# Two-layer attention network on one core: the second layer's value projection moves from the first layer's loop into the second's, and the first layer's instruction orders are laid out anew

## The chip, the core and the metric

The kernel runs on one core of a Trainium2 chip. A core has five engines with instruction streams of their own: TensorE (PE, matrix products and transposes into the eight PSUM banks), VectorE (DVE), ScalarE (ACT), GpSimd (POOL) and SyncE (SP, which here only issues DMAs). They run in parallel and meet at semaphores; each engine works through its own list strictly in order, so an instruction that waits holds up all behind it. The metric is the device time of one execution in microseconds, lower is better.

## The reference

32 independent sequences of 128 tokens with 128 features go through two layers. All is fp32.

```python
x = x + xattn0(layernorm(x), ctx)      # 16 heads of 8, key mask, biases
x = x + moe(layernorm(x))              # top-2 of 8 experts, 128 -> 512 -> 128, relu
x = x + xattn1(layernorm(x), ctx)      # 16 heads of 64, query mask:
#   k, v = split(ctx @ Wkv);  q = x @ Wq;  softmax(q k^T / 8 + mask) v @ Wout + bout
x = x + ffn(layernorm(x))              # 128 -> 512 -> 128, relu, biases
```

`v = ctx @ Wkv[:, 1024:]` of the third line is the second layer's value projection: for each sequence a product of the 128x128 context with a 128x1024 matrix. It depends on the context alone, not on `x`, and so can be computed at any time.

## The kernel before

The rows of `x` stay in SBUF for the whole run (`X`, 32 tiles of 128x128). There are three phases.

**Phase 0, the first layer's attention and the router.** Each engine runs `step0(n, p)` from `over_steps`, a software pipeline: at step n, parts of several sequences stand in one list. `p` is the parity of n and picks one of two buffers. The steps in the middle are loops of two steps per iteration, cut into four loops between which `late_loads` issues bulk weight loads on SyncE. For a sequence the chain is: normalise (`norm_*`, GpSimd does the power of -1/2), transpose (`transpose_in`, bank 5, read to `XCT` by `read_xct` on ScalarE), project to keys and queries (`project`, bank 4), split both into a high and a low part (`PARTS`; `kh`, `kl` and `ql` on VectorE, `qh` on ScalarE), write them to DRAM and read them back in a block layout (`KBD`, `QS`; SyncE), four score groups of four heads (`scores`, lines 1042 and 1045, banks 0 and 1 in turn), row maxima (line 748), exponentials with row sums (line 580), transpose of the probabilities (`transpose_unit`, line 1027, banks 2 and 3 in turn, read by `read_PT` on VectorE, line 759, and ScalarE, line 588), 16 value products (`values`, line 1057), scaling by the reciprocal sums (`RB`, `RTS`, `OT0`, line 851), output projection (line 1140), residual sum (line 857). The router then normalises the row alone (`XND`), transposes it, computes expert logits, top-8, index and one-hot (`lgs`, `top8`, `topi`, `tope`, `hot1`, `chosen`), counts places (`place`, `next_row`), and GpSimd scatters the normalised rows (copied to `XK`) to DRAM, line 519.

In the same loop the second layer's value projection is computed: `second_layer_v(f)`, line 1074, two matmuls of 128x512 per sequence into bank 6. ScalarE copies each half to `V_OUT` (`read_v_half`, line 595) and SyncE writes the 512 KB to the DRAM tensor `second_layer_values` (line 410). The two halves stand in TensorE's list behind the second score group and behind the third; both use bank 6, so the second waits for ScalarE's copy of the first.

**Phase 1, the experts**, over the scattered rows. **Phase 2, the second layer**, `step1(n, p)` with the same kind of pipeline: 16 key and query projections (`project_y`, line 1192, banks 4 to 6), scores in two groups (line 1206), row maxima, exponentials, scaling on GpSimd (line 316), transposes, values (line 1225, banks 5 and 6), output projection (line 1275, bank 7), and the feed-forward part (lines 1263 and 1280, both bank 4). SyncE reads the stored values of each sequence back to `V1` (line 454).

The order of instructions on each engine is written out by hand in `step0` and `step1`. The semaphores used below are named after what they count: `a["e"]` exponential groups, `a["pv"]` value groups, `a["qh"]` high parts of queries, and so on.

Of the kernel before, what the change touches and what calls it, by code (L numbers as in the profile page):

```python
# [20 lines left out]
FP32 = mybir.dt.float32  # L21
# [69 lines left out]

def is_first(n):
    return isinstance(n, int) and n == -1
# [9 lines left out]
def build(nc, x, ctx_in, mask_keys, mask_queries, wq0, bq0, wk0, bk0, wv0, bv0, wo0, bo0,  # L103
          gate_w, moe_w1, moe_w2, wq1, wkv1, wout1, bout1, ffn_w1, ffn_b1, ffn_w2, ffn_b2, out, c_dram, xs, ys):
    ctx = ExitStack()
    with ctx:  # L106
# [6 lines left out]
        v_dram = nc.dram_tensor("second_layer_values", (NB, P, INNER), FP32, kind="Internal").ap()  # L113
# [68 lines left out]
        V_OUT = wide[:, PAIRS:2 * PAIRS, :].rearrange("p k s -> p (k s)")  # L182
# [52 lines left out]
        wq_scaled, ld_kv = sem("wq_scaled"), sem("ld_kv")  # L235
# [14 lines left out]
        a = names("a", common + "kq v0 qc qh ql kc kh kl kw qw vc qs bd s mx e rd rb t pt0 pt1 pv rt rts oN o x pj pjv vst")  # L250
        c = names("c", common + "mask0 mask1 v0 v1 y yc s mx e rd nm t pt0 pt1 pv oT o x")
# [78 lines left out]
        def _(sp):  # L330
# [4 lines left out]
            def early_loads(n):  # L335

                if n == -3:
# [6 lines left out]
                    sp.dma_start(wv1[:], wkv1[:, INNER:]).then_inc(ld_kv, 16)  # L344
# [13 lines left out]
            def late_loads(k):  # L358
# [20 lines left out]
                if k == 4:  # L379
                    sp.dma_start(wout[:], wout1.rearrange("(c p) d -> p c d", p=P)).then_inc(ld_w1, 16)  # L380

            def step0(n, p):

                if exists(n + 1):
                    m = n + 1
                    if isinstance(n, int) and m < 2:
                        sp.wait_ge(bd_zeroed, m + 1)
                    wait_apart(sp, (a["kw"], 16 * (m + 1)), (a["s"], NU * (m - 1)))
                    for j in range(G):
                        rows = spread(1 - p, 1).rearrange("(g j x) s -> j x g s", g=NU, j=G)[j]  # L390
                        sp.dma_start(KBD[32 * j:32 * j + 32, 1 - p, :, j, :].bitcast(FP32), rows).then_inc(a["bd"], 16)
                    wait_apart(sp, (a["qw"], 32 * (m + 1)))
                    sp.dma_start(QS[:, 1 - p, :, :].bitcast(FP32),
                                 spread(1 - p, 0).rearrange("(g x) s -> x g s", g=NU)).then_inc(a["qs"], 16)
                if exists(n + 3):
                    load_ctx(sp, a, n + 3, 1 - p)
                if isinstance(n, int):
                    early_loads(n)
                if exists(n + 2):
                    m = n + 2  # L400
                    wait_apart(sp, (a["kl"], m + 1), (a["bd"], 16 * G * (m - 1)))
                    sp.dma_start(spread(p, 1).rearrange("(c o i) s -> c o i s", o=2, i=2),
                                 PARTS[:, 0:2, :].unsqueeze(1).broadcast_to([P, 2, 2, P])).then_inc(a["kw"], 16)
                    wait_apart(sp, (a["ql"], m + 1), (a["qs"], 16 * (m - 1)))
                    for o in range(2):
# [903 lines left out]
```

## Time and profile before

| | us |
|---|---|
| three runs, median (lowest, highest) | 1075.23 (1074.84, 1075.88) |
| the profiled execution, its own time | 1078.77 |
| its span, first to last instruction | 1076.9 |

| engine | busy us | share of the span |
|---|---|---|
| PE (matmul) | 942.5 | 88% |
| PEld (weight load, beside PE) | 805.1 | 75% |
| DVE | 671.6 | 62% |
| ACT | 596.2 | 55% |
| POOL | 416.6 | 39% |

A line of a timeline shows the start in us, the length in us, the engine, the line of the kernel, the operation, what is written and read, how many instructions were merged, and in brackets the idle time before it and what ended it. Records overlap, as an engine starts an instruction before the last one has left its pipeline; what an instruction costs its engine is therefore the distance between starts. An fp32 matmul has two records. "<-issue" stands for time in which the profile shows no releaser.

### The profile page before, as it was taken

The numbers are of one execution on the slowest core, as the hardware profiler recorded it, in microseconds if no ns is written. First come the engines' busy times: TensorE is split into PE (matmuls) and PEld (weight loads), VectorE is DVE, ScalarE is ACT, GpSimd is POOL, SyncE is SP. The second block draws the span as 40 slices with busy tenths as digits, with TensorE's granted clock in tenths as the row PEclk, the third lists the DMA queues.
The fourth block names the chain that finished last, engine by engine and source line by source line (L and its number), as shares of the span: only waits on it lengthen the run. The fifth ranks groups of instructions, "written<-read, shape, count | busy, mean of one in ns | idle before, by whom it ended". The sixth has DMA issues, their size and how long they took to land. (4 is left out here: it accounts for less than half of the span.)

```text
span 1076.9 us, 30219 instructions
## 1 busy us (share of the span) xinstructions
PE 942.5 (88%) x8590; PEld 805.1 (75%) x8590; DVE 671.6 (62%) x2173; ACT 596.2 (55%) x2537; POOL 416.6 (39%) x670
## 2 busy tenths in 40 slices
PE   5888788888888873799995799999999999999987
PEld 3556566555665652799995688999999999999986
DVE  5667767767777666122222667777777777777763
ACT  2867777767777670133331455556555655555552
POOL 4123333333333333011113455555555555555531
PEclk9989999989999895799997899999999999999998
DMA  5764475554754522122222011111111111111110
GB/s 152 223 196 148 132 234 163 181 151 132 232 167 139 149 93 62 44 69 68 69 68 71 30 56 51 45 56 59 59 56 56 59 41 52 59 59 59 56 45 9
DMA packets 110658, 103.56 MB, mean 96 GB/s; under 512 B 11759, under 2 KB 96563, under 8 KB 110614
## 3 DMA queue, kind: packets, MB, share of 16 engines
q1 hardware_dynamic: 102958, 89.14, 26.9%
q0 software_dynamic: 5776, 12.99, 3.8%
q10 hardware_dynamic: 1880, 0.92, 0.3%
q8 instruction: 19, 0.31, 0.1%
q14 instruction: 25, 0.20, 0.1%
HBM read 56.45 MB, written 46.56 MB: 96 GB/s over the span
## 5 line engine op out<-in xcount | busy, mean ns | idle before, releaser
L580 ACT ACTIVATE PR<-bank,nmx 128x128 f32<-128x128 f32 x1024 | 362.4, 375 | 130.3 <-issue 114.5
L580 ACT ACTIVATION_READ_ACCUMULATOR PR<-bank,nmx 128x1 f32 x1024 | 218.4, 213 | 0.0
L748 DVE TENSOR_REDUCE nmx<-bank 128x4 f32<-128x512 f32 x256 | 170.0, 685 | 69.8 <-PE bank L1045 60.4
L316 POOL TENSOR_TENSOR PR<-PR,rden 128x512 f32<-128x512 f32 x128 | 134.0, 1047 | 92.5 <-DVE rden L753 91.5
L1027 PE MATMUL bank<-ident,PR 128*128 128x128 f32 x1024 | 152.5, 277 | 0.3 <-DVE YT L759 0.3
L1027 PEld LDWEIGHTS bank<-ident,PR 128*128 128x128 f32 x1024 | 121.0, 143 | 29.9 <-issue 25.9
L1192 PE MATMUL bank<-XCT,wqk 128*128 128x128 f32 x1024 | 123.8, 281 | 0.9 <-ACT XCT L572 0.9
L1192 PEld LDWEIGHTS bank<-XCT,wqk 128*128 128x128 f32 x1024 | 120.6, 197 | 1.6 <-ACT XCT L572 1.6
L572 ACT ACTIVATE XCT<-bank 128x256 f32<-128x256 f32 x64 | 24.7, 385 | 160.9 <-PE bank L1019 160.9
L1074 PE MATMUL bank<-wv,XCT 128*128 128x512 f32 x128 | 74.2, 663 | 37.9 <-ACT wide L595 37.9
L649 ACT ACTIVATE H<-bank 128x512 f32<-128x512 f32 x70 | 41.9, 598 | 107.5 <-PE bank L1162 107.5
L519 POOL DMA_INDIRECT expert_inputs<-wide,scat_idx x64 | 66.0, 1032 | 79.2 <-DVE scat_idx L824 69.1
L917 DVE COPY YT<-bank 128x512 f32<-128x512 f32 x128 | 85.6, 687 | 10.5 <-PE bank L1192 7.8
L276 POOL TENSOR_SCALAR veps<-mv 128x1 f32<-128x1 f32 x128 | 29.0, 226 | 160.0 <-DVE mv L292 100.6
L1206 PE MATMUL bank<-YT 64*128 64x128 f32 x1024 | 74.8, 286 | 6.5 <-ACT PR L580 2.8
L550 POOL DMA_INDIRECT QF<-expert_outputs,gidx x64 | 65.5, 1024 | 36.5 <-POOL gidx L547 24.4
L279 POOL TENSOR_TENSOR rstd<-veps,expo 128x1 f32<-128x1 f32 x128 | 73.3, 572 | 15.7 <-POOL veps L276 10.2
L1045 PE MATMUL bank<-KBD,QS 128*128 128x512 f32 x128 | 76.6, 599 | 0.0
L1206 PEld LDWEIGHTS bank<-YT 64*128 64x128 f32 x1024 | 62.5, 188 | 15.6 <-issue 10.9
L1162 PE MATMUL bank<-PR,w 128*128 128x128 f32 x560 | 70.1, 279 | 0.5 <-DVE PR L900 0.5
L1169 PE MATMUL bank<-w,H 128*128 128x128 f32 x560 | 69.3, 278 | 0.0
L533 POOL DMA_DIRECT2D expert_outputs<-PR x35 | 19.1, 545 | 128.7 <-DVE PR L908 128.7
(178 smaller groups left out, 1810.2 us busy)
## 6 DMA issues: line engine op xcount, KB each, us to landing
second_layer_values<-wide SPq DMA_DIRECT2D x32, 512.0 KB, 2.8
wide<-second_layer_values SPq DMA_DIRECT2D x32, 512.0 KB, 3.3
expert_outputs<-HF SPq DMA_DIRECT2D x32, 256.0 KB
expert_outputs<-HF SPq DMA_DIRECT2D x64, 128.0 KB
KBD<-expert_outputs SPq DMA_DIRECT2D x128, 64.0 KB
QS<-expert_outputs SPq DMA_DIRECT2D x32, 256.0 KB
PR<-expert_inputs SPq DMA_DIRECT2D x36, 128.0 KB, 2.1
expert_outputs<-PR POOLq DMA_DIRECT2D x35, 128.0 KB, 2.0
```

What stands on the lines that cost most here:

```text
L279: nc.gpsimd.tensor_tensor(rstd[:, p, :], veps[:, p, :], expo[:], ALU.pow).then_inc(s["rstd"], 1)
L316: nc.gpsimd.tensor_tensor(unit, unit, rden[:, p, G * g:G * g + G].unsqueeze(2).broadcast_to([P, G, P]), ALU.mult).then_inc(s["nm"], 1)
L580: last = nc.scalar.activation(PR[:, g, j * P:(j + 1) * P], S_BANK[g % 2][:, j * P:(j + 1) * P], ACT.Exp, bias=nmx[:, p, h:h + 1], accum_ou ...
L748: nc.vector.tensor_reduce(nmx[:, p, G * g:G * g + G], S_BANK[g % 2][:].rearrange("p (j k) -> p j k", j=G), AXX, ALU.max, negate=True).then ...
L917: nc.vector.tensor_copy(YT[:, q, G * g:G * g + G, :].rearrange("p h s -> p (h s)"), Y_BANK[g][:]).then_inc(c["yc"], 1)
L1027: last = nc.tensor.transpose(T_BANK[g % 2][:, j * P:(j + 1) * P], PR[:, g, j * P:(j + 1) * P], ident[:])
L1045: mm(S_BANK[g % 2][:], QS[:, p, g, :], KBD[:, p, g, :, :].rearrange("p j s -> p (j s)"), start=False, stop=True, skip_group_check=True).th ...
L1074: mm(bank[6][:], XCT[:, q, 1, :], wv1[:, 512 * f:512 * f + 512], start=True, stop=True).then_inc(a["pj"], 1)
L1162: last = mm(bank[k][:, i * P:(i + 1) * P], w1[:, e, i * P:(i + 1) * P], XT[:, k, :], start=True, stop=True)
L1169: last = mm(bank[4 + k][:, 0:P], H[:, k, i, :], w2[:, e, i, :], start=(i == 0), stop=(i == HC - 1))
L1192: last = mm(Y_BANK[g][:, j * P:(j + 1) * P], wqk1[:, 1 - g // 2, chunk * P:(chunk + 1) * P], XCT[:, q, 1 - g // 2, :], start=True, stop=True)
L1206: mm(S_BANK[r][:, j * P:(j + 1) * P], QT1[half, p, chunk, :], KT1[half, p, chunk, :], start=(j == 0), stop=False, skip_group_check=True)
```

## The change

- The second layer's value projection leaves phase 0 with its two matmuls, two ScalarE copies, the DRAM tensor, its write and its semaphores. Phase 2 gets it: `project_v(half)` writes bank 5 and bank 6, and ScalarE's `read_v(half)` copies them to `V1`. The read from DRAM goes. The weights `wv1` are loaded after the last cut of phase 0.
- In phase 2 the feed-forward's second product moves from bank 4 to bank 7, ahead of the output projection, which then waits for `d["x"]`; the second score group stands behind the transposes of the first unit.
- Phase 0 gets new orders on all five engines. For sequence n the output projection, the residual sum and the router's transpose go to a later step; ScalarE's step begins with the query part, `RTS`, the third and fourth exponentials and a transposed unit of the sequence before; ScalarE and SyncE run three steps longer.

The diff, cut to its core (TensorE's, ScalarE's and SyncE's loop bodies and phase 2):

```diff
@@ SyncE, step0
+                    wait_apart(sp, (a["ql"], n + 2), (a["qs"], 16 * (n)))
+                    for o in range(2):
+                        sp.dma_start(spread(q, 0).rearrange("(c o i) s -> o c i s", o=2, i=2)[o],
+                                     PARTS[:, 2 + o, :].unsqueeze(1).broadcast_to([P, 2, P])).then_inc(a["qw"], 16)
...
-                if exists(n + 1):
-                    wait_apart(sp, (a["pjv"], 2 * n + 4))
-                    sp.dma_start(v_dram[n + 1], V_OUT).then_inc(a["vst"], 16)
@@ ScalarE, step0 after the change
+                if exists(n + 1):
+                    act.wait_ge(a["qc"], n + 2)
+                    wait(act, a["qw"], 32 * (n + 1))
+                    nc.scalar.activation(PARTS[:, 2, :].bitcast(FP32R), QC, ACT.Copy).then_inc(a["qh"], 1)
+                if exists(n - 2):
+                    act.wait_ge(a["rt"], n - 1)
...
+                if exists(n - 1):
+                    exponentials(a, n - 1, q, 2)
+                    exponentials(a, n - 1, q, 3)
+                    read_PT(a, n - 1, 1)
...
+                if exists(n + 2):
+                    read_xct(a, n + 2, p, True, a["v0"], n + 1)
                 if exists(n):
                     exponentials(a, n, p, 0)
                     exponentials(a, n, p, 1)
...
-                if exists(m):
-                    read_v_half(m, 0)
                 if exists(n - 1):
                     read_PT(a, n - 1, 3)
@@ ScalarE, step1
                 if exists(n):
                     exponentials(c, n, p, 3)
+                if exists(m):
+                    read_v(0)
+                if exists(n):
                     read_PT(c, n, 1)
+                if exists(m):
+                    read_v(1)
@@ TensorE, step0: the new order, waits left out
+                    nc.tensor.transpose(M_BANK[:, 0:P], XND[:], ident[:]).then_inc(rt["tr"], 1)
...
+                    mm(M2_BANK[:, 0:P], OT0[:, p, :], wo0T[:], start=True, stop=False)
...
+                    scores(n, p, 0)
...
+                    mm(bank[4][:, 2 * P:3 * P], XCT[:, p, 1, :], wv0T[:], start=True, stop=False)
...
+                    transpose_in(a, n + 2, p, True)
+                if exists(n):
+                    scores(n, p, 1)
+                if exists(n - 1):
+                    transpose_unit(a, n - 1, 2)
...
-                if exists(m):
-                    second_layer_v(0)
@@ TensorE, step1
+                def project_v(half):
+
+                    if exists(n - 1):
+                        wait(pe, c["oT"], 2 * (n - 1) + half + 1)
+                    else:
+                        pe.wait_ge(c["yc"], NU * m + half + 2)
+                    mm(bank[5 + half][:], XCT[:, q, 1, :], wv1[:, 512 * half:512 * half + 512], start=True, stop=True).then_inc(c["v"], 1)
...
+                if exists(m):
+                    project_v(0)
                 if exists(n):
                     transpose_unit(c, n, 1)
-                if exists(n - 1):
+                if exists(n - 2):
+                    wait(pe, d["hr"], n - 1)
+                    wait(pe, d["xct"], n - 1)
+                    for kk in range(HC):
+                        mm(bank[7][:, 0:P], H[:, 0, kk, :], f2[:, kk, :], start=(kk == 0), stop=False)
...
+                if exists(m):
+                    project_v(1)
+                if exists(n - 1):
+                    wait(pe, c["oT"], 2 * n)
                     if exists(n - 2):
-                        wait(pe, d["xct"], n - 1)
+                        wait(pe, d["x"], n - 1)
```

VectorE's new order in phase 0, in words: router transpose copy (`XDT`), residual sum, input statistics, row maxima 0, reciprocal of the sums, statistics of the residual, row maxima 1, `place` and `next_row`, transposed unit 2, `KC`, `picked`, high and low part of the keys, `lgs`, `QC`, top-8, `XND`, index search, row maxima 2, low part of the queries, `slot_f`, `XN`, `tope` and `hot1`, row maxima 3, `scat_idx`, `OT0`, transposed unit 0, `chosen`. GpSimd's: `RB`, router normalisation, copy to `XK`, input normalisation, two scatters.

## Rows read from the trace of the kernel before

**Rows 1.** Windows (stretch, length, busy PE PEld DVE ACT POOL, clock, DMA share, GB/s): both layers.

```profile
21.30:394.40 373.10, 308.68 (x2353) 222.84 (x2354) 259.37 (x993) 280.36 (x1236) 119.67 (x230) 0.97 0.57 172
...
584.00:1076.90 492.90, 471.98 (x4896) 428.20 (x4896) 341.01 (x926) 260.50 (x1184) 248.94 (x347) 0.97 0.16 51
```

**Rows 2.** Windows of 25 sequences each: PE, PEld, DVE, ACT, POOL, clock, DMA.

```profile
101.00:401.00 300.00, 247.45 (x1932) 179.36 (x1928) 210.40 (x833) 225.42 (x992) 102.51 (x195) 0.98 0.54 163
640.00:1000.00 360.00, 359.19 (x3813) 327.55 (x3813) 264.71 (x722) 203.11 (x925) 197.29 (x275) 1.00 0.17 55
```

**Rows 3.** Timeline of PE in the second layer: the first score group of two steps.

```profile
797.97 1.16 PE L1206 MATMUL bank<-YT 64*128 64x128 f32 x16
...
812.38 1.16 PE L1206 MATMUL bank<-YT 64*128 64x128 f32 x16
```

**Rows 4.** Timeline of DVE in one step of the first layer: its waits.

```profile
310.53 0.69 DVE L748 TENSOR_REDUCE nmx<-bank 128x4 f32<-128x512 f32 x1 [0.30 <-PE bank L1045]
...
318.04 0.69 DVE L748 TENSOR_REDUCE nmx<-bank 128x4 f32<-128x512 f32 x1 [1.42 <-PE bank L1045]
...
320.51 0.29 DVE L851 TENSOR_TENSOR OT<-bank,RTS 128x128 f32<-128x128 f32 x1 [0.29 <-PE bank L1057]
...
321.95 0.29 DVE L857 TENSOR_TENSOR X<-bank,X 128x128 f32 x1 [0.89 <-PE bank L1141]
322.28 0.69 DVE L748 TENSOR_REDUCE nmx<-bank 128x4 f32<-128x512 f32 x1
```

**Rows 5.** Timeline of PE around that step of the first layer.

```profile
311.52 1.02 PE L1074 MATMUL bank<-wv,XCT 128*128 128x512 f32 x2
312.38 0.38 PE L1066 MATMUL bank<-XCT,wqkT 128*128 128x128 f32 x2
...
315.77 1.13 PE L1074 MATMUL bank<-wv,XCT 128*128 128x512 f32 x2 [1.14 <-ACT wide L595]
316.73 0.60 PE L1027 MATMUL bank<-ident,PR 128*128 128x128 f32 x4
...
317.93 1.97 PE L1057 MATMUL bank<-YT 128*64 128x128 f32 x32
319.83 0.66 PE L1027 MATMUL bank<-ident,PR 128*128 128x128 f32 x4
...
321.30 0.44 PE L1140 MATMUL bank<-wo0T,OT 128*128 128x128 f32 x2
```

**Rows 6.** Timeline of ACT in that step.

```profile
315.12 0.60 ACT L595 ACTIVATE wide<-bank 128x512 f32<-128x512 f32 x1
...
316.09 0.37 ACT L580 ACTIVATE PR<-bank,nmx 128x128 f32<-128x128 f32 x1
...
317.37 0.23 ACT L580 ACTIVATION_READ_ACCUMULATOR PR<-bank,nmx 128x1 f32 x1
```

**Rows 7.** Timeline of SyncE: the reads of the block layout.

```profile
319.43 1.86 SPq L391 DMA_DIRECT2D KBD<-expert_outputs  x4
321.46 0.39 SPq L393 DMA_DIRECT2D QS<-expert_outputs  x1
```

**Rows 8.** Timeline of POOL: second scatter of a step, and the copy behind it.

```profile
318.81 0.96 POOL L519 DMA_INDIRECT expert_inputs<-wide,scat_idx  x1 [0.30 <-issue]
322.06 0.29 POOL L524 COPY wide<-XND 128x128 f32<-128x128 f32 x1 [2.29 <-DMA expert_inputs<-wide,scat_idx]
```

**Rows 9.** Waits from 101 to 401 us: total, times, longest.

```profile
POOL wide L524 <- DMA expert_inputs<-wide,scat_idx: 65.3, 25, 6.3
```

**Rows 10.** Timeline of ACT: one instruction per step, around the longest step.

```profile
203.88 0.31 ACT L608 ACTIVATE HF<-QF 128x128 fp32r<-128x128 f32 x1 [0.16 <-DVE QF L797]
...
218.79 0.31 ACT L608 ACTIVATE HF<-QF 128x128 fp32r<-128x128 f32 x1 [3.17 <-DVE QF L797]
```

**Rows 11.** Windows around a fall of the granted clock, columns as above.

```profile
215.00:218.00 3.00, 0.63 (x4) 0.66 (x4) 1.02 (x6) 0.62 (x4) 1.27 (x4) 0.72 1.20 183
218.00:221.00 3.00, 2.13 (x4) 0.80 (x4) 2.49 (x11) 2.21 (x9) 0.79 (x2) 0.50 0.16 36
```

More of the change, by code:

```diff
@@ L89, in loads, with is_sequence, upto @@
     return 8 * (m - p) + 16
+def is_sequence(k, m):
+    return isinstance(m, int) and m == k
+def upto(m, each=1, item=0):
+    count = each * m + item + 1
+    return min(count, each * NB) if isinstance(m, int) else count
 def is_first(n):
@@ L652, in step1, with read_v @@
                 q, m = 1 - p, n + 1
+                def read_v(half):
+                    act.wait_ge(c["v"], 2 * m + half + 1)
+                    wait(act, c["pv"], NU * (m - 1))
+                    nc.scalar.activation(V1[:, q, 8 * half:8 * half + 8, :], bank[5 + half][:].rearrange("p (h d) -> p h d", h=8),
+                                         ACT.Copy).then_inc(c["vc"], 1)
                 def read_heads(half):
@@ L762, in step0 @@
             def step0(n, p):
-                q, l = 1 - p, n + 2
+                q = 1 - p
                 if isinstance(n, int):
                     weights_and_masks(n)
+                if exists(n - 3):
+                    dve.wait_ge(rt["tr"], n - 2)
+                    wait(dve, rt["lg"], n - 3)
+                    nc.vector.tensor_copy(XDT[:], M_BANK[:, 0:P]).then_inc(rt["xct"], 1)
+                if exists(n - 2):
+                    dve.wait_ge(a["o"], n - 1)
+                    xrow = X[:, bass.ds(n - 2, 1), :].rearrange("p o d -> p (o d)")
+                    nc.vector.tensor_tensor(xrow, M2_BANK[:, 0:P], xrow, ALU.add).then_inc(a["x"], 1)
+                if exists(n + 3):
+                    norm_dve_stats(dve, a, None, n + 3, q)
+                if isinstance(n, int) and n == -2:
+                    bias_rows()
                 if exists(n):
@@ L970, in step1 @@
                     norm_dve_stats(dve, c, None, n + 2, p)
+                if exists(n - 2):
+                    dve.wait_ge(d["y"], n - 1)
+                    wait(dve, out_stored[p], loads(n - 4, p))
+                    nc.vector.tensor_tensor(acc[:, p, :], bank[7][:, 0:P],
+                                            X[:, bass.ds(n - 2, 1), :].rearrange("p o d -> p (o d)"),
+                                            ALU.add).then_inc(d["x"], 1)
                 if exists(n + 2):
@@ L1015, in transpose_in @@
                     pe.wait_ge(s[f"ctx{p}"], loads(m, p))
[L1016 removed]
+                if m_free is not None:
+                    wait(pe, m_free, m_count)
                 last = nc.tensor.transpose(M_BANK[:, 0:P], XN[:, p, :], ident[:])
@@ L1078, in step0 @@
+                    mm(bank[4][:, 2 * P:3 * P], ones3[:], brow[:, 0, :], start=False, stop=True).then_inc(a["v0"], 1)
+                if exists(n + 2):
+                    wait(pe, a["x"], upto(n - 2))
+                    if isinstance(n, int):
+                        wait(pe, a["rts"], upto(n - 2))
+                        wait(pe, a["xct"], upto(n + 1))
+                    transpose_in(a, n + 2, p, True)
+                if exists(n):
+                    scores(n, p, 1)
                 if exists(n - 1):
@@ L1102, in step0 @@
+                    nc.tensor.transpose(M2_BANK[:, 2 * P:3 * P], RB[:], ident[:]).then_inc(a["rt"], 1)
+                if exists(n - 3):
+                    pe.wait_ge(rt["xct"], n - 2)
+                    wait(pe, rt["next"], upto(n - 4))
+                    if isinstance(n, int):
+                        wait(pe, rt["xct"], upto(n - 3))
+                        wait(pe, rt["lgc"], upto(n - 4))
                     mm(M_BANK[:, 0:NE], XDT[:], gw[:], start=True, stop=True).then_inc(rt["lg"], 1)
```

332 lines of the change are left out of this document (137 added, 195 removed).

## The prediction

> **What bounds the kernel now.** I read the stages first, because one average over the span would mix them. Cut at the first and last sequence's first score group and at the start of the second layer, the table of stretches gives 373.1 us for 31 sequences of the first layer (12.04 us each) and 492.9 us for the second layer, ends included [rows 1]. The steady part of each is in [rows 2]: 25 sequences lie in each of its stretches.
>
> The second layer is bound by TensorE: 359.19 of 360 us busy, at full clock [rows 2]. Busy time of matmuls is modelled, so I checked it by starts: the same matmul group starts at 797.97 and 812.38, a step of 14.41 us [rows 3], and the steps between differ by a few hundredths. The other engines are busy 264.71/25 = 10.6 us (VectorE), 8.1 (ScalarE) and 7.9 (GpSimd) per sequence [rows 2].
>
> The first layer is bound by no engine alone. Per sequence TensorE is busy 247.45/25 = 9.9 us, ScalarE 9.0, VectorE 8.4, GpSimd 4.1 [rows 2]. So I read the timelines of one step for what each engine waits on. VectorE's step from 310.53 to 322.28 is 11.75 us, and three waits on TensorE stand in it: 1.42, 0.29 and 0.89 us, 2.60 in all [rows 4]. That leaves 9.15 us of work and short waits on VectorE's own results. The step before it reads the same way: 12.25 us with five waits of 3.40 us in all, so 8.85. The mean is 9.0. The largest wait (row maxima of the fourth score group) has its cause in TensorE's timeline: the second half of the second layer's value projection waits 1.14 us for ScalarE to copy the first half out of its only bank [rows 5], and that copy stands behind the copy of the query part in ScalarE's order. The fourth scores are queued behind that matmul.
>
> **The change part by part.**
>
> *Second layer, added work.* Each sequence gains two matmuls of 128x512 in fp32. In the trace the pair of records of one half takes 0.86 us from start to next start (311.52 to 312.38), 0.96 where it follows an idle engine (315.77 to 316.73) [rows 5]. So 2 x 0.86 = 1.72 us per sequence. They land on the engine that has no hole: 14.41 becomes 16.13. The first projection stands in the prologue (about +1.5 us, as the first scores are behind it) and the second in a hole while the first sequence's exponentials end; I count 30 x 1.72 + 1.5 = 53.1. The two copies added to ScalarE (0.49 us each: such a copy and a second one of its size take 315.12 to 316.09 from start to next start [rows 6]) make it 8.1 + 1.2 = 9.3 us busy in 16.1 (0.60 us of record each): covered, if each is done when its bank is wanted. The first half's bank (bank 5) still holds the attention output of the previous sequence; its copy follows the third group of exponentials, and I work it out to end within 0.1 us of when TensorE comes to it. The feed-forward output now goes to bank 7 ahead of the output projection; its hidden activations are ready about when TensorE arrives, since the added half-projection and one transpose unit stand between. I take 0 to 0.1 us a step for both, 2 us in all. At the end of the layer the last output projection now waits for the one-but-last feed-forward sum: +1 us. Sum for the second layer: +53 + 2 + 1 = **+56 us**, bounds +52 (nothing but the matmuls of 30 steps) and +63 (0.3 us of wait in each step).
>
> *Second layer, removed.* The read of 512 KB per sequence from DRAM, with its issue on SyncE, is gone. No engine waits for it in the steady part: **0**. DMA is busy a share of 0.17 there [rows 2].
>
> *First layer, removed work.* Per sequence 1.72 us of TensorE, two copies of ScalarE (1.0 us of issue), one DMA of 512 KB. TensorE has at most 9.9 - 1.7 = 8.2 us left, ScalarE 8.0. The 1.42 us wait of VectorE on the fourth scores has no cause any more. If that were all, the step would be 12.0 - 1.5 = 10.5 us.
>
> *First layer, new orders.* They take the projection of the output, the residual sum and the router's transpose one step later, and put the third and fourth exponentials of a sequence at the head of ScalarE's next step. What this does to VectorE's other waits (0.29 for the head outputs, 0.89 for the residual [rows 4]) I worked out by walking one step of the new orders over all engines with the old durations. Start at the second group of exponentials of sequence n, time 0. It is read out at 1.5 (316.09 to the end at 317.60 [rows 6]); ScalarE copies the transposed unit 3 of n-1 until 2.0; the 16 value matmuls run 1.90 us (317.93 to 319.83 [rows 5]) to 3.9; VectorE can scale the head outputs at 4.2 (0.29 us), and it comes to that instruction at about 4.5, so it does not wait. The output projection gives the residual at 0.65 us from its start (321.30 to 321.95 [rows 4, 5]), at about 5.5; VectorE is busy until then with the copy of transposed unit 0, `chosen` and `XDT`. Input statistics (0.5) and the row maxima of n+1 (0.69 each) follow. Through TensorE and ScalarE alone this ring closes in 8.1 us. VectorE's own list is longer: the 9.0 us found above, minus about 0.2 us of waits on its own results, which are now filled by other instructions (top-8 and index search), is 8.8. So VectorE is the next bound. I add 0.2 for waits that the walk can't see (the rings of 8.1 and 8.8 are close). Step: **9.0 us**, bounds 8.6 (work without self-waits, 8.4, and 0.2) and 10.5 (only the value wait is gone).
>
> Queues that instructions are moved past. SyncE: the query part's write now stands ahead of the reads of the K layout in the next step, and waits for VectorE's last part. The reads are issued from 319.43 to 321.29 and the read of Q at 321.46 [rows 7]; with an estimate of 2.3 to 4 us for each landing, the lower end from the scatter's [rows 8], I find Q in place some 2 to 3 us before the scores want it. GpSimd: the copy of the normalised rows waits until the scatter before has landed, 2.3 us after its issue ends (318.81 + 0.96 to 322.06 [rows 8]). VectorE's next normalisation waits for that copy. This ring is 2.4 us of scatter issue, 0.3 of copy, 2.9 of VectorE's list from `XND` to `scat_idx` and the landing: 7.9 us, under 9.0. But the longest such wait was 6.3 us [rows 9], which makes the ring 11.9 us; it comes where bulk weights are loaded. I therefore keep the lengthened steps of before as they are: five steps of 12.8 to 14.9 us exceed 11.85 us by 9.6 us in all; the longest is 203.88 to 218.79 [rows 10]. About 4 us more are VectorE's own set-up steps (mask rows, zeroing), which were partly hidden and are not when it is the bound.
>
> Sum of the first layer: 31 x 9.0 + 9.6 + 4 = 292.6 against 373.1: **-80 us** (rounded). The start (query write behind the row moves, +0.5) and the drain (same chain of router steps) I take as 0 within 2 us.
>
> *Total:* -80 + 56 = -24. The profiled run took 1078.8 us and the median is 1075.2, 0.3% less; the difference is carried to the median: 1075.2 - 24 = **1051 us**.
>
> *A rule weighed.* TensorE stands still for 1.14 us in a step and the clock stays up: 0.97 of full speed over the first layer [rows 1]. It fell to 0.72 and 0.50 only in 215 to 221 us, after a stretch in which TensorE was busy 0.63 of 3 us [rows 11]. The Trainium skill, "TensorE: Matmul & The Clock Gate", section "Why this matters for your kernels", warns against idle gaps between bursts of matmuls, as the array falls back to half clock. That speaks against taking work from a layer with idle TensorE. It is a rival below; the sum goes by the row, since the new step is shorter and TensorE's share of it is not lower: by distances of starts it is occupied 8.8 of 12 us, and 7.1 of 9 without the projection.
>
> **The rivals.**
>
> A. *The new orders gain only the value wait.* Another wait replaces the two others: scatter ring, K/Q round trip, or register arithmetic ahead of waits. Step 10.5 us: 31 x 10.5 + 13.6 = 339, -34 us; total +22: **1097 us**. It decides from a step of 9.79 us on, where 31 x 9.79 + 13.6 = 317 gives back all 56 us. For it: the rings of 7.9, 8.1 and 8.8 us lie close, and a landing of 4 us makes the scatter ring 9.6. Against it: typical landings were 2.3 us with more DMA traffic than will be left. Steps of 9.8 and more: 0.19.
>
> B. *Step shorter than 8.7*, VectorE without self-waits and fewer lengthened steps: 31 x 8.5 + 10 = 273.5, -100; total -44: **1031 us**. 0.06.
>
> C. *The projection is cheap in the second layer.* Weight loads keep their unit busy 327.55 of 360 us [rows 2], 1.30 us free per step. If that were the room, 1.72 us would cost 0.42, or 13 us in all: 1075.2 - 80 + 13 + 3 = **1011 us**. Against it: matmuls start back to back. 0.02. The rule behind it is in the Trainium skill, "Perfetto Trace Analysis", section "Identifying the Most-Contended Engine": headroom of TensorE is judged by the load of weights, not by matmul busy time.
>
> D. *Half clock in the first layer.* TensorE's 7.1 us become 14.2, a step of about 14.5: 31 x 14.5 + 13.6 = 463, +90; total +146: **1221 us**. By the gate's rule above; the trace shows such drops only after long stops. 0.02 (inside the slower cases).
>
> **How the numbers follow.** Forecast, step 8.7 to 9.4: 1042 to 1064, chance 0.58. Step 9.4 to 9.75: 1064 to 1075, 0.13, of which 0.04 is within 0.2% (2 us), about what a measurement of this kernel can tell from no change. A with D: 0.21 slower. B and C: 0.08. Faster 0.58 + 0.09 + 0.08 = 0.75, same 0.04, slower 0.21. The range leaves out B's lower half and C below (0.05), and the upper half of A with D above (0.13): **1032 to 1088**.
>
> **What would show it.** The second layer's step 16.1 to 16.3 us with TensorE busy throughout; a hole at the half-projections means the banks came late. The first layer's step 9.0 us with VectorE idle under 0.5 us of it. VectorE waiting at the normalisation for GpSimd means the scatter ring, at row maxima 0 and 2 for scores means the exponentials or the K/Q round trip; TensorE's granted clock under 0.9 in the first layer means D. The prediction is wrong if two of VectorE's waits stay, or if the walk missed a wait on the same engine pair in the other direction.

## The result, and the profile after

The change makes the kernel faster: 1036.69 us (median of 4 runs, 1036.06 to 1037.69) against 1075.46 (4 runs, 1074.84 to 1075.88), a ratio of 0.9641, 95% interval 0.9624 to 0.9658. The forecast was 1051 us, 14 us too high, within its range of 1032 to 1088. The profiled execution took 1036.79 us with a span of 1035.2.

Where the 41.7 us of span between the two profiled executions went, cut at VectorE's first and last scaling of head outputs (`OT0`) and at the second layer's first `XCT` copy:

| stretch | before | after | difference |
|---|---|---|---|
| start to first `OT0` | 41.25 | 37.69 | -3.6 |
| first to last `OT0`, 31 steps of the first layer | 371.7 | 279.4 | -92.3 |
| last `OT0` to second layer (router's end, experts) | 173.7 | 173.1 | -0.7 |
| second layer to the end | 490.2 | 545.1 | +54.9 |

The page of the changed kernel gives, engine by engine, busy us, share of the span and number of instructions:

```profile
PE 936.0 (90%) x8590; PEld 800.7 (77%) x8590; DVE 661.9 (64%) x2173; ACT 586.9 (57%) x2537; POOL 415.6 (40%) x670
```

The second layer is still bound by TensorE. Windows of the changed kernel (columns as in [rows 1]); the first is 200 us of the first layer, the second has the stretch of [rows 2]:

```profile
101.00:301.00 200.00, 182.24 (x1602) 143.19 (x1602) 175.42 (x734) 168.33 (x828) 91.07 (x172) 0.97 0.57 169
640.00:1000.00 360.00, 357.04 (x3472) 307.28 (x3468) 237.18 (x641) 205.61 (x875) 170.31 (x237) 1.00 0.05 15
```

The timeline of PE shows both half-projections (L1182) in their places with no wait in the whole step; it is 784.60 - 768.45 = 16.15 us long, against 14.41 in [rows 3]:

```profile
762.18 1.16 PE L1268 MATMUL bank<-XDT,f 128*128 128x128 f32 x8
763.20 1.12 PE L1182 MATMUL bank<-wv,XCT 128*128 128x512 f32 x2
764.16 0.60 PE L1024 MATMUL bank<-ident,PR 128*128 128x128 f32 x4
764.60 1.11 PE L1278 MATMUL bank<-f,H 128*128 128x128 f32 x8
765.55 0.22 PE L1279 MATMUL bank<-brow,ones 128*128 128x128 bf16 x1
765.60 1.08 PE L1182 MATMUL bank<-wv,XCT 128*128 128x512 f32 x2
766.52 1.95 PE L1289 MATMUL bank<-wout,wide 128*128 128x128 f32 x16
...
768.45 1.16 PE L1210 MATMUL bank<-YT 64*128 64x128 f32 x16
...
784.60 1.16 PE L1210 MATMUL bank<-YT 64*128 64x128 f32 x16
```

In the first layer the waits of [rows 4] are gone from the usual step. The same stretch of VectorE's list, from the scaled heads (L846) over the residual (L768) to the row maxima, two steps' maxima 8.34 us apart (the next pair is 8.52 apart, 8.43 on average), has no bracket. From 101 to 301 us VectorE waits 2.8 us for scores, in six pieces, and 13.0 us for GpSimd's copy of the normalised rows, also in six:

```profile
248.64 0.28 DVE L846 TENSOR_TENSOR OT<-bank,RTS 128x128 f32<-128x128 f32 x1
248.84 0.68 DVE L754 COPY YT<-bank 128x512 f32<-128x512 f32 x1
249.43 0.16 DVE L851 TENSOR_TENSOR chosen<-hot 128x8 bf16<-128x8 f32 x1
249.51 0.29 DVE L764 COPY XDT<-bank 128x128 f32<-128x128 f32 x1
249.71 0.28 DVE L768 TENSOR_TENSOR X<-bank,X 128x128 f32 x1
249.91 0.28 DVE L277 BATCH_NORM_STATS2 stats<-X 128x6 f32 x1
250.28 0.18 DVE L279 BATCH_NORM_AGGREGATE mv<-stats 128x2 f32<-128x6 f32 x1
250.41 0.69 DVE L743 TENSOR_REDUCE nmx<-bank 128x4 f32<-128x512 f32 x1
...
258.75 0.69 DVE L743 TENSOR_REDUCE nmx<-bank 128x4 f32<-128x512 f32 x1
```

Four steps between 100 and 300 us are long: 11.1, 11.2, 12.0 and 11.4 us. POOL's timeline shows why in the longest. The copy of the normalised rows (L513) waits 4.56 us for the scatter to land, and VectorE's next `XND` waits for that copy; the window says what else was moving, 301 GB/s with the DMA engines 0.94 busy, just behind a block of weight loads. The write of the keys' and queries' parts is late by the same block (ScalarE's copy of the query part waits 2.63 us for it), but that wait ends at 227.50 us, before the scatter's:

```profile
221.22 0.96 POOL L521 DMA_INDIRECT expert_inputs<-wide,scat_idx  x1 [0.30 <-issue]
...
227.97 0.29 POOL L513 COPY wide<-XND 128x128 f32<-128x128 f32 x1 [4.56 <-DMA expert_inputs<-wide,scat_idx]
```

```profile
219.00:228.00 9.00, 8.26 (x75) 6.22 (x73) 5.60 (x23) 6.34 (x32) 3.17 (x6) 1.00 0.94 301
```

Behind this stop the granted clock falls. TensorE is busy 0.33 us of the three from 228 to 231 us, and then runs at half clock:

```profile
231.20:234.20 3.00, 2.90 (x12) 2.47 (x12) 2.59 (x11) 2.28 (x11) 2.07 (x2) 0.50 0.54 156
```

The same is read behind the other three long steps (0.50 at 122, 177 and 286 us), and the step behind each takes 9.0 to 9.7 us in place of 8.59.

### The profile page after: what moved, and what is told of

It reads as the page before. It is cut to its first block and busy times, and to the rows that moved or that the text cites. A ratio compares the mean times of both kernels' runs of the same rounds, so it can differ in the third digit from the quotient of the medians.

```text
span 1035.2 us, 29985 instructions
## 1 busy us (share of the span) xinstructions
PE 936.0 (90%) x8590; PEld 800.7 (77%) x8590; DVE 661.9 (64%) x2173; ACT 586.9 (57%) x2537; POOL 415.6 (40%) x670
## 5 line engine op out<-in xcount | busy, mean ns | idle before, releaser
L578 ACT ACTIVATION_READ_ACCUMULATOR PR<-bank,nmx 128x1 f32 x1024 | 223.4, 218 | 0.0
L1196 PE MATMUL bank<-XCT,wqk 128*128 128x128 f32 x1024 | 121.6, 278 | 0.9 <-ACT XCT L570 0.9
L1196 PEld LDWEIGHTS bank<-XCT,wqk 128*128 128x128 f32 x1024 | 118.4, 194 | 1.6 <-ACT XCT L570 1.6
L521 POOL DMA_INDIRECT expert_inputs<-wide,scat_idx x64 | 66.0, 1032 | 97.7 <-DVE scat_idx L841 86.8
L285 POOL TENSOR_SCALAR veps<-mv 128x1 f32<-128x1 f32 x128 | 29.2, 228 | 165.5 <-DVE mv L301 150.6
L1042 PE MATMUL bank<-KBD,QS 128*128 128x512 f32 x128 | 78.7, 615 | 0.0
L1289 PEld LDWEIGHTS bank<-wout,wide 128*128 128x128 f32 x512 | 61.9, 192 | 15.8 <-issue 13.7
L1182 PE MATMUL bank<-wv,XCT 128*128 128x512 f32 x128 | 70.0, 630 | 1.0 <-ACT wide L648 1.0
```

Source lines behind the costliest of these rows:

```text
L521: nc.gpsimd.indirect_dma_start(xs, bass.IndirectOffsetOnAxis(scat_idx[:, p, k:k + 1], 0), XK[:, p, :], None).then_inc(rt[f"sc{p}"], 16)
L578: last = nc.scalar.activation(PR[:, g, j * P:(j + 1) * P], S_BANK[g % 2][:, j * P:(j + 1) * P], ACT.Exp, bias=nmx[:, p, h:h + 1], accum_ou ...
L1042: mm(S_BANK[g % 2][:], QS[:, p, g, :], KBD[:, p, g, :, :].rearrange("p j s -> p (j s)"), start=False, stop=True, skip_group_check=True).th ...
L1182: mm(bank[5 + half][:], XCT[:, q, 1, :], wv1[:, 512 * half:512 * half + 512], start=True, stop=True).then_inc(c["v"], 1)
L1196: last = mm(Y_BANK[g][:, j * P:(j + 1) * P], wqk1[:, 1 - g // 2, chunk * P:(chunk + 1) * P], XCT[:, q, 1 - g // 2, :], start=True, stop=True)
```

## The experiments

Three groups of four runs; each group ran on one chip beside the kernel before. "Steps" is first to last `OT0`, 31 steps; "usual" their median; "long" is the excess over the median of the steps more than 0.5 us above it; "2nd" the mean step of the second layer's steady part. Of the changed kernel one execution lies outside the groups, and one is in group 3; groups 1 and 2 have none beside them, so their comparisons with it cross groups.

| run | group | time us | ratio to before (95%) | steps | usual | long | 2nd |
|---|---|---|---|---|---|---|---|
| before | | 1075.46 | | 371.7 | 11.70 | 12.7 | 14.41 |
| changed | | 1036.69 | 0.9641 (0.9624, 0.9658) | 279.4 | 8.59 | 16.8 | 16.15 |
| value_only | 1 | 1110.71 | 1.036 (1.0298, 1.0422) | 354.3 | 10.72 | 29.2 | 16.15 |
| orders_only | 1 | 1009.05 | 0.9408 (0.9354, 0.9461) | 304.7 | 9.24 | 21.9 | 14.40 |
| v_half | 1 | 1053.41 | 0.981 (0.9749, 0.9872) | 293.0 | 8.71 | 26.6 | 16.15 |
| late_loads | 1 | 1035.88 | 0.9659 (0.9604, 0.9714) | 277.3 | 8.71 | 9.0 | 16.15 |
| dve_extra | 2 | 1054.02 | 0.9796 (0.9748, 0.9844) | 285.3 | 8.84 | 15.4 | 16.5 |
| act_extra | 2 | 1052.90 | 0.9786 (0.9745, 0.9826) | 283.4 | 8.83 | 14.4 | 16.5 |
| half_projection | 2 | 1052.20 | 0.9787 (0.9738, 0.9836) | 282.6 | 8.81 | 14.7 | 16.3 |
| orders_fine | 2 | 1005.33 | 0.933 (0.93, 0.9359) | 296.8 | 9.75 | 1.7 | 14.40 |
| changed again | 3 | 1040.06 | 0.9697 (0.9674, 0.9721) | 281.9 | 8.80 | 15.2 | 16.15 |
| dve_two | 3 | 1047.82 | 0.9778 (0.9738, 0.9817) | 291.3 | 9.15 | 13.8 | 16.15 |
| orders_again | 3 | 1006.01 | 0.9385 (0.9362, 0.9409) | 301.2 | 9.23 | 19.4 | 14.40 |
| orders_fine_again | 3 | 992.83 | 0.9253 (0.9223, 0.9283) | 286.3 | 9.23 | 3.7 | 14.40 |

### The two parts apart: value_only and orders_only

`value_only` takes `second_layer_v`, `read_v_half` and the DRAM write out of the old `step0` and gives it the changed `step1`. `orders_only` is the changed `step0` with the two matmuls, two ScalarE copies and a write per step, and the old `step1`:

```diff
@@ value_only, TensorE's old step0 (ScalarE and SyncE likewise)
-                if exists(m):
-                    second_layer_v(0)
...
-                if exists(m):
-                    second_layer_v(1)
@@ orders_only, TensorE's new step0
+                    pe.wait_ge(a["pjv"], 2 * n + 1)
+                    mm(bank[6][:], XCT[:, p, 1, :], wv1[:, 512:1024], start=True, stop=True).then_inc(a["pj"], 1)
                     scores(n, p, 0)
...
+                    wait(pe, a["pjv"], 2 * (n + 1))
+                    mm(bank[6][:], XCT[:, q, 1, :], wv1[:, 0:512], start=True, stop=True).then_inc(a["pj"], 1)
                 if exists(n):
                     scores(n, p, 2)
```

> The value projection alone is moved to the second layer as in the changed kernel; the first layer keeps the orders of the kernel before, with the projection, its copies and its write taken out. Theory (each engine's order sets the step): TensorE still waits for ScalarE's value copy and VectorE's list still has its gaps, so the first layer's step is about 10.5 us against 12.04 before and 8.43 in the changed kernel (mean without lengthened steps), the second layer's step 16.15; total about 1097 us. Rival (the orders are worth nothing, the removed work did it all): step about 8.5, total about 1037 us, the same as the changed kernel.

> The changed kernel's first-layer orders, but both halves of the second layer's value projection stay in the first layer (through a bank of their own, copied by ScalarE, written to DRAM), and the second layer is that of the kernel before. Theory (lists): TensorE gets 2 x 0.86 us and ScalarE 2 x about 0.6 us per step on top of a step of 8.43, in which each had 0.5 to 1.3 us to spare, so the step goes to 9.0 to 9.3 us; the second layer's step is again 14.41; total 1036.7 - 55 + 31 x 0.7 = about 1003 us, 33 us below the changed kernel. Rival (the orders only work once the projection is out): the step stays above 10.5 us, total about 1046 us, above the changed kernel.

With the old orders the usual step falls only to 10.72 us, 16.5 us more than before is lost in long steps, and the projection's 55 us in the second layer are not earned back: 1110.71 us, slower than before by 3.6%. That is rival A's condition (orders that gain nothing else), and 14 us beyond its price; the waits are others than the three it names. TensorE waits for VectorE at the router's bank, and VectorE for TensorE at the scores and the residual (101 to 380 us; engine, line, waited for, total, times, longest), and the granted clock from 101 to 301 us is 0.92:

```profile
PE bank L1083 <- DVE next_row L774: 34.7, 24, 5.1
PE bank L1093 <- DVE lgs L803: 24.9, 23, 1.3
```

```profile
DVE nmx L738 <- PE bank L1035: 28.3, 44, 1.4
DVE X L847 <- PE bank L1120: 22.0, 24, 1.3
```

```profile
101.00:301.00 200.00, 156.24 (x1294) 119.87 (x1290) 147.52 (x589) 136.81 (x654) 73.33 (x138) 0.92 0.47 137
```

The new orders alone give 1009.05 us, better than the whole change. In the third group the same kernel takes 1006.01 us against 1040.06 for the changed kernel beside it: moving the projection costs 34 us on top of the new orders, 19.4 us gained in the 31 steps and 4.0 ahead of them, 57.6 lost in the second layer. TensorE has no gap in a usual step of it (14 us of the first layer):

```profile
217.00:231.00 14.00, 14.00 (x126) 10.75 (x125) 12.70 (x55) 13.27 (x65) 5.33 (x12) 1.00 0.59 198
```

### What a half-projection costs in the second layer: v_half and half_projection

`v_half` computes, stores and reads back heads 0 to 7 in the first layer's way, and drops `project_v(0)`. `half_projection` drops `project_v(1)` and copies half 0 twice; the values of heads 8 to 15 are not computed.

```diff
@@ TensorE, step1: v_half drops the first, half_projection the second
-                if exists(m):
-                    project_v(0)
...
-                if exists(m):
-                    project_v(1)
```

> The changed kernel, with half 0 of the value projection in the first layer (one 128x512 matmul, one ScalarE copy, one DRAM write per step; read back in the second layer) and half 1 in the second. Theory (VectorE's list bounds the first layer's step, with 0.62 us of ScalarE and over 0.86 us of TensorE to spare): first layer's step 8.43 to 8.6 us, so +0 to +5 us there; second layer's step 15.3 (16.15 - 0.86), -27 us there; total 1010 to 1015 us. Rival (TensorE or ScalarE bounds the first layer's step as closely as VectorE does): step 9.0 or more, total 1027 us or more.

> The changed kernel, but the second layer projects only half 0 of the values and copies it twice, so that heads 8 to 15 get the wrong values: the second 128x512 matmul of each step is left out, the copies stay. It is the mirror of the run that kept half 1 and left half 0 out, whose step stayed at 16.15 us because TensorE then waited 0.78 us for VectorE's relu where half 0 had stood. Theory (half 0 covers that wait, half 1 covers nothing): the second layer's step falls by the whole 0.86 us to 15.3, total about 1037 - 27 = 1010 us. Rival (something else holds the second layer's step at 16.15, and no matmul less helps): total about 1037 us.

Both theories on the second layer fell. Without half 0 its step stays at 16.15 us: TensorE reaches the feed-forward's second product (here L1300) 0.86 us earlier and waits 0.78 us there for VectorE's relu:

```profile
763.35 1.16 PE L1292 MATMUL bank<-XDT,f 128*128 128x128 f32 x8
764.34 0.60 PE L1041 MATMUL bank<-ident,PR 128*128 128x128 f32 x4
765.73 1.16 PE L1300 MATMUL bank<-f,H 128*128 128x128 f32 x8 [0.78 <-DVE H L974]
```

Without half 1 it is 15.95 us in its undisturbed steps: the output projection comes early to bank 7, which VectorE's feed-forward sum (L968) has not read yet:

```profile
723.92 1.12 PE L1278 MATMUL bank<-f,H 128*128 128x128 f32 x8
724.87 0.22 PE L1279 MATMUL bank<-brow,ones 128*128 128x128 bf16 x1
725.57 0.68 PE L1287 MATMUL bank<-wout,wide 128*128 128x128 f32 x4 [0.48 <-DVE QF L968]
```

So each half-projection covers a wait that shows in the changed `step1` when it is taken out: the two together cost 1.74 us a step against the old order, and either one beside the other 0.00 or 0.20 us. No run has the changed `step1` with neither half, or the old one with one half; by TensorE's work the latter would take 14.41 + 0.86 = 15.3 us (an estimate), so what `v_half` could have gained with another `step1` stays open.

In the first layer `v_half`'s usual step of 8.71 us, between the 8.59 and 8.80 of the changed kernel, shows that TensorE and ScalarE had room for one half. Its long steps cost 10 us more, and their waits are of another kind: ScalarE cannot overwrite `V_OUT` before the values' write to DRAM has landed (12.0 us from 101 to 301 us).

```profile
ACT wide L603 <- DMA second_layer_values<-wide: 12.0, 5, 3.3
```

### What bounds the first layer's step: dve_extra, act_extra, dve_two and a control

```diff
                     row_max(a, n, p, 1)
+                    nc.vector.tensor_copy(wide[:, 16:20, :], ident[:].unsqueeze(1).broadcast_to([P, 4, P]))   # dve_two: twice
```
```diff
+                    nc.scalar.activation(wide[:, 20:24, :], ident[:].unsqueeze(1).broadcast_to([P, 4, P]), ACT.Copy)
                     exponentials(a, n - 1, q, 2)
```

> The changed kernel with one more VectorE instruction in each first-layer step: a 128x512 copy from SBUF to an unused SBUF buffer, after the maximum of group 1, that nobody waits for. Theory (VectorE's list sets the first layer's step, since it shows no idle time there): every step grows by what the copy takes, about 0.6 us as the 128x512 copies of the trace, so 32 x 0.6 = +19 us; total about 1056 us. Rival (TensorE and VectorE are both near the bound and some waiting is hidden in VectorE's packed records): growth well under half, total below 1046 us.

> The changed kernel with one more ScalarE instruction in each first-layer step: a 128x512 copy from SBUF to an unused SBUF buffer, ahead of the exponentials of group 2, where ScalarE waits 0.62 us in every step. Theory (VectorE bounds, ScalarE has that gap): the copy takes about 0.5 us and fills the gap, total 1037 to 1040 us. Rival (ScalarE's exponentials lie on the ring that sets the step): +0.5 us in each step, +16 us, total about 1053 us.

> The changed kernel unaltered, on the chip of the three runs below, as their control: the runs with one extra instruction, and with half a projection, all showed every second step of the second layer at 16.9 us where the changed kernel's first profile has 16.28, and a first-layer step of about 8.8 us against 8.59, whatever had been edited. If that belongs to the execution and not to the edits, this run can show it too (1045 to 1050 us); if it belongs to the edits, this run is at 1037 us again, with 16.28 and 8.59.

> As the run with one extra VectorE copy per first-layer step (0.33 us of VectorE's time), but with two such copies, 0.66 us. Theory (VectorE's list of 8.4 to 8.5 us bounds the step, with at most 0.25 us of waiting in it): the step is 9.05 to 9.2 us, 0.45 to 0.6 above the control of this call, the first layer 14 to 19 us longer. Rival (the step is set by a ring through TensorE and VectorE, which has room for what is put beside it): step under 0.3 us above the control, first layer under 9 us longer.

The totals of group 2 are misleading: in all three kernels derived from the changed one every second step of the second layer was longer (in `act_extra` 16.81 us in place of 16.15 between starts of TensorE's first score group). `dve_extra` and `act_extra` do not touch that code, and their second layers take 553.5 and 555.2 us to the end, against 545.2 in the control of group 3. The last section says what the traces of group 2 have in common. The first layers of the group can be compared with each other. Against `half_projection`, whose first layer is the changed kernel's, the ScalarE copy added 0.8 us to 31 steps: it has room, as the theory said, though the total of 1052.90 us reads like the rival's. One VectorE copy (0.33 us from start to start, not the 0.6 I expected of it) added 2.8 us. That neither theory foresaw, and the waits of `half_projection` say why: VectorE waited there for TensorE's counts, 0.23 us at a time, at just the place of the copy (120 to 300 us). These counts (L1098) came 0.9 us after their matmul's record had ended; in the control of group 3 they came 0.03 us after it, and VectorE waits there twice, 0.4 us in all. So the room that the copy found belongs to group 2.

```profile
DVE place L784 <- PE bank L1098: 4.2, 18, 0.6
```

Two copies against the control: usual step 9.15 against 8.80, so 0.35 us for 0.67 of copies, and the 31 steps +9.5 us, just above the rival's 9 and short of the theory's 14 to 19. VectorE is then full:

```profile
249.80 0.69 DVE L743 TENSOR_REDUCE nmx<-bank 128x4 f32<-128x512 f32 x1
...
254.04 0.42 DVE L782 COPY wide<-ident 128x512 f32<-128x512 f32 x1
254.38 0.41 DVE L783 COPY wide<-ident 128x512 f32<-128x512 f32 x1
254.71 0.15 DVE L786 TENSOR_TENSOR place<-bank,next_row 128x8 f32<-128x8 f32 x1
...
258.94 0.69 DVE L743 TENSOR_REDUCE nmx<-bank 128x4 f32<-128x512 f32 x1
```

9.14 us less the two copies (254.04 to 254.71, 0.67) is a list of 8.47 us. The changed kernel's usual step lies 0.1 to 0.3 us above it; in the control these are waits of `XND` for GpSimd's copy, 14 in the 200 us against 4 with the two copies, ten of the 14 being of 0.2 to 0.5 us (control first, then dve_two; total, times, longest):

```profile
DVE XND L308 <- POOL wide L513: 13.6, 14, 3.5
```

```profile
DVE XND L308 <- POOL wide L513: 8.1, 4, 2.5
```

So VectorE's list is the floor, as forecast, and the ring through the scatter lies 0.1 to 0.3 us above it.

### The long steps: late_loads, orders_fine and its repeat

`late_loads` moves the calls of `late_loads(k)`, all but the load of `X`, behind SyncE's last step, with the loop cut as before. `orders_fine` is `orders_only` with a cut at every iteration and a piece of the loads at each:

```diff
@@ late_loads
-            over_steps(sp, step0, -3, NB + 3, 3, 4, late_loads)
+            over_steps(sp, step0, -3, NB + 3, 3, 4, first_loads)
+            for k in range(5):
+                late_loads(k)
@@ orders_fine
-    cuts = list(range(loop_start, loop_end, 3)) + [loop_end] if between else [loop_start, loop_end]
+    cuts = list(range(loop_start, loop_end, every)) + [loop_end] if between else [loop_start, loop_end]   # SyncE: every=1
+                if 1 <= k <= 8:
+                    sp.dma_start(w1[:, k - 1, :], moe_w1[k - 1]).then_inc(ld_ffn, 16)
+                    sp.dma_start(w2[:, k - 1, :, :], moe_w2[k - 1].rearrange("(c p) d -> p c d", p=P)).then_inc(ld_ffn, 16)
```

> The changed kernel, but the bulk loads of the expert, feed-forward and second-layer weights, which SyncE issues between its stretches of the first layer's loop, are all issued after the last first-layer step; the cuts of the loop stay. Theory (the lengthened steps come from the loads, which slow the scatter and the spreads): the steps of 9.2 to 12.4 us fall to 8.4 to 8.6, first layer 281.6 to about 266 us; the expert stage may start up to 15 us later, since its weights come late. Rival (the cut of the loop itself costs the time): the lengthened steps stay where they are and the first layer keeps 281 us.

> The kernel with the changed first-layer orders and the value projection in the first layer (1009.05 us), and SyncE's bulk loads cut into eleven pieces of about 0.5 MB, issued every two steps, in place of four blocks of 1 to 2 MB every six. Theory (a block of loads delays the landing of the scatter, and only a delay of several us outlasts the slack of the row buffer): the lengthened steps of 10.5 to 15.2 us, 21.9 us above the usual 9.24 in all, lose over half of that: first layer about 12 us shorter, total 995 to 999 us. Rival (the same bytes cost the same time wherever they are put): total about 1009 us.

> The kernel with the changed first-layer orders and the value projection in the first layer once more, beside the control. If the chip of this call gives the same step as before (9.24, TensorE without a gap), total 1007 to 1010 us, 28 us or more below the control. If its step goes to 9.5 to 9.8 us, the 9.75 us of the run with finely cut loads belongs to the chip and not to the loads.

> The same with the bulk loads cut into eleven pieces, on the same chip as the run before it. Theory (fine loads take away the lengthened steps and cost nothing else): 12 us or more below the run with the loads in four blocks. Rival (the bytes cost the same spread or in a block, since the run of the other call had no lengthened step but 9.75 us in every step): within 4 us of it.

`late_loads`: the four long steps between 100 and 300 us fall to 8.2 to 9.0 us, so the loads made them and not the cuts, and the granted clock there is 1.00 in place of 0.97. But the total is unchanged, and the 31 steps take 277.3 us against 279.4, where the theory had 15 us less: the usual step is 8.71, the long step near the start stays (13.1), the block now meets the last two scatters, whose steps take 11.4 and 10.7 us, and the second layer starts 3 us later after the last heads:

```profile
301.59 0.29 POOL L518 COPY wide<-XND 128x128 f32<-128x128 f32 x1 [4.48 <-DMA expert_inputs<-wide,scat_idx]
...
313.32 0.29 POOL L518 COPY wide<-XND 128x128 f32<-128x128 f32 x1 [4.82 <-DMA expert_inputs<-wide,scat_idx]
```

With the projection in the first layer the long steps have a second cause beside the scatter. In `orders_again` ScalarE waits for the values' write behind a block, 4.17 us at most, and TensorE and VectorE wait behind it:

```profile
ACT wide L603 <- DMA second_layer_values<-wide: 12.0, 3, 4.2
```

Cut finely, the loads cost almost nothing. In group 3, side by side, the usual step is 9.23 us with either layout, that wait is 5.7 us in all, the long steps shrink from 19.4 to 3.7 us, and the time from 1006.01 to **992.83 us**, 7.5% below the kernel before and 4.5% below the changed one in that group. TensorE is busy 197.98 of 200 us of the first layer at full clock:

```profile
101.00:301.00 200.00, 197.98 (x1663) 153.35 (x1663) 176.06 (x724) 182.07 (x852) 91.36 (x172) 1.00 0.70 222
```

In group 2 the same kernel had 9.75 us in every step and 1005.33 us. Group 3's chip was the same one. What differed in the traces is TensorE's counts (last section): in group 2 the count of the context's transpose (L1022) came 0.6 us after the matmul's record ended, in group 3 0.01 us after it, and only in group 2 did ScalarE wait for it (9.2 us from 101 to 301 us, 18 times). Why the counts were late is open.

## Why the prediction was right, point by point

- **Second layer, +56.** Measured +54.9; step 16.15 us for 16.1 to 16.3. The mechanism held: the work landed on an engine without a gap. The closeness of the sum is partly luck. From first to last first score group the 31 steps grew by 48.2 us (448.8 to 497.0) and the start by 0.2, for the 53.1 of the sum; the banks were in time in every step, so the 2 us of waits did not come; and the end grew by 6.4 us (34.1 to 40.5), for 1. In the last steps, where no projection is left, TensorE waits 0.78 us for VectorE's relu and 0.47 for its feed-forward sum, the same waits that the half-projections cover elsewhere (v_half, half_projection). I had not seen them. The profiled execution of before was itself 2.6 us longer in this stretch than `orders_again`, which runs the same second layer (490.2 against 487.6 us); against that the addition is 57.5 us.
- **First layer's step, 9.0.** Measured 8.43 us where VectorE is packed, 8.59 as the median. The mechanism held (VectorE's list bounds; the waits of [rows 4] go), and the term was mis-sized. I took 9.0 us of list and short waits, subtracted 0.2 for the short waits and added 0.2 for unseen ones; the list itself measures 8.47 (dve_two), so the short waits were worth 0.5, and what lies above the list is 0.12. 31 x 0.41 = 13 us, about the size of the error of the total, though other errors below cancel beside it.
- **Lengthened steps, 9.6 us as before.** They cost 16.8. Four of them come from the scatter behind a block of loads; with a shorter step the same delay sticks out further. That took back 7 us. Behind each of the four the clock was at 0.50 for a stretch, and the next step was 0.4 to 1.1 us longer; the sum has no term for that.
- **Set-up steps +4, start +0.5, drain 0.** The start came 3.6 us earlier and the drain 0.7; no 4 us of set-up show, and the steps under the median give another 3.7. With these the 31 steps come out at 292.6 - 12.7 + 7.2 - 4 - 3.7 = 279.4 us. The medians differ by 38.8 us and not by 41.7, mostly because the profiled execution of before was 3.3 us slower than its median.
- **"If only the removed work counted, 10.5 us."** value_only: 10.72, and 29 us of long steps. The step was right within 0.2 us, but not the reason given for it: waits of VectorE for the scores remain (28.3 us from 101 to 380 us). Rival A's condition, orders that bring nothing else, is just that kernel, and it is slower than before. The new orders were worth 67 us in group 3 (before to orders_again), the removal 19 us.
- **Rival C** fell: the unit that loads weights was busy 307.28 of 360 us and free 2.4 us a step, while TensorE had no gap. The Trainium skill names that unit's busy share as one of two measures of TensorE's headroom ("Perfetto Trace Analysis", section "Identifying the Most-Contended Engine"). Judged by it the added work would have cost the 0.42 us a step of rival C; it cost 1.74, so the runs do not agree.
- **Rival D** did not come as priced: the clock is 0.97 over the first layer, as before. It came in part, behind the long steps. The reading that it was built on was too narrow: in the kernel before the clock was at 0.50 not only around 217 to 223 us but also from 59.5 to 66 and from 363.5 to 369.5 us. In the changed kernel it is at 0.50 behind each of the four long steps, in `late_loads`, without them, 1.00 from 101 to 301 us, and in value_only 0.92, with TensorE busy 156 of 200 us. The Trainium skill warns of idle gaps between bursts ("TensorE: Matmul & The Clock Gate", section "Why this matters for your kernels"); these runs agree in direction.

## What to carry to other kernels

Before moving work off an engine that waits, lay out the orders so that the waits go, and only then ask what the work costs where it stands: here the first was worth 67 us, and the move that came with it lost 34 of them. A matmul that covers a wait is free to keep and worth nothing to remove; read what stands behind it in the same list. Spread bulk loads in pieces over a loop that has a short DMA round trip in its ring; here a block was paid in the ring at both places where it was put. Compare kernels only within a group that has its own control: in one group of this case a disturbance of the executions was as large as the effects under test.

## What was not expected of the hardware

- Behind a block of loads of 2 MB the scatter's second DMA landed 5.8 us after its issue ended, against 2.3 us one step before, at 301 GB/s.
- In group 2 VectorE's copy of the transposed unit 0 waited 0.85 us for TensorE in every second step of the second layer, where the changed kernel's did not wait, with TensorE's instructions before it at the same times. First act_extra, then the changed kernel:

```profile
806.96 0.69 DVE L755 COPY w<-bank 128x512 f32<-128x512 f32 x1 [0.85 <-PE bank L1231]
```

```profile
793.90 0.68 DVE L754 COPY w<-bank 128x512 f32<-128x512 f32 x1
```

It is not the chip (the control of group 3 ran on the same one without it) and not an extra VectorE instruction (dve_two has none of it). The semaphore events of the traces say more. VectorE's copy waits for the first count of the value products (L1231 in act_extra). In act_extra that count came at 806.94, 2.22 us after the first of these matmuls started; in the changed kernel it came 1.10 us after. From 640 to 900 us the three kernels of group 2 with the changed `step1` have 1.5 and 2.2 us in turn, orders_fine of the same group has 1.1 to 1.3, and every run of groups 1 and 3 has 1.10 in every step. So it goes with the executions of that group and not with the edits. Why the counts come late is open.

- The profiled execution of before has late counts too. In the step of [rows 4] the four counts of the value products (L1057) came together between 320.31 and 320.49 us, when the last of the matmuls had ended by its record at 319.89. VectorE's wait of 0.29 us there ends with them. In the changed kernel the same counts come 0.02 us after their records. One execution of before was profiled, so how much of the gain over it is orders and how much is the absence of late counts is not shown; the times of the runs beside each other (1072.99 and 1006.01 us in group 3) stand.
